# Sixteen matmuls of the identity on TensorE ahead of the first projection

## What is computed

```python
Q = (x @ Wq.T).reshape(b, n, H, R); K = (x @ Wk.T).reshape(b, n, H, R)
V = (x @ Wv.T).reshape(b, n, H, d)
attn = softmax(einsum('bnhr,bmhr->bhnm', Q, K), axis=-1)
x = layernorm(x + einsum('bhnm,bmhd->bnd', attn, V))
h = silu(tlin(x, w1_w, w1_s)) * tlin(x, w2_w, w2_s)
h = gelu(tlin(h, h1_w, h1_s)); h = gelu(tlin(h, h2_w, h2_s))
x = layernorm(x + tlin(h, w3_w, w3_s))
```

## Time and profile before

| | |
|---|---|
| median of three runs | 1031.53 us (1029.31 to 1032.75) |
| the profiled execution | 1031.28 us, its span 1029.4 us |
| TensorE busy | 984.3 us (96%) |
| ScalarE, VectorE, GpSimd busy | 859.1, 827.1, 513.0 us |
| mean granted TensorE clock | 0.980 |

### The profile page before, as it was taken

How to read it: one execution, slowest core, us unless ns; L and a number is a source line. 1 busy time by engine, 2 the same in 40 slices (tenths; PEclk the granted TensorE clock), 3 DMA queues, 4 the chain that set the end, 5 groups by cost and what they waited for, 6 DMA issues and landing times.

```text
span 1029.4 us, 19535 instructions
## 1 busy us (share of the span) xinstructions
PE 984.3 (96%) x6465; PEld 816.5 (79%) x6465; DVE 827.1 (80%) x1827; ACT 859.1 (83%) x1992; POOL 513.0 (50%) x509
## 2 busy tenths in 40 slices
PE   4887999999999999999999999999999999999976
PEld 3676888888888888888888888888888888888844
DVE  4695778887888988788898878889887888878754
ACT  5574998989899898989989898998989899898632
POOL 1591545544455554545555454555545454554623
PEclk9898999999999999999999999999999999999978
DMA  5000000000100000010000001000000100000000
GB/s 184 11 3 21 2 11 12 21 11 2 31 2 22 12 21 11 1 32 2 21 12 21 12 2 32 2 22 11 22 11 2 32 1 12 11 12 11 12 0 21
DMA packets 21749, 17.81 MB, mean 17 GB/s; under 512 B 1040, under 2 KB 17936, under 8 KB 21648
## 3 DMA queue, kind: packets, MB, share of 16 engines
q1 hardware_dynamic: 21648, 16.53, 5.3%
HBM read 12.33 MB, written 4.19 MB: 16 GB/s over the span
## 4 chain that ended last, share of the span: by engine, by line
PE 91%; DVE 4%; ACT 2%; issue 2%; DMA 0%; POOLq 0%; SPq 0%; DVEq 0%; POOL 0%; ACTq 0%
PE bank L852 13%; PE bank L958 13%; PE bank L959 13%; PE bank L846 12%; PE bank L848 11%; PE bank L847 11%; PE bank L891 11%; PE bank L938 3%; PE bank L939 3%; ACT prob L383 1%; DVE pt_lo L196 1%; DMA wk_in<-in_wk_t 0%; DVE neg_max L600 0%; DVE t_lo L196 0%; DVE v_lo L196 0%
## 5 line engine op out<-in xcount | busy, mean ns | idle before, releaser
L248 POOL TENSOR_TENSOR prob<-prob,inv_total 128x512 f32<-128x512 f32 x256 | 267.8, 1057 | 185.0 <-DVE inv_total L606 185.0
L383 ACT ACTIVATE prob<-bank,neg_max 128x256 f32<-128x256 f32 x512 | 237.9, 480 | 4.1 <-DVE neg_max L600 3.4
L196 DVE TENSOR_TENSOR pt_lo<-bank,pt_hi 128x512 fp32r<-128x512 f32 x256 | 175.4, 685 | 46.3 <-ACT pt_hi L199 41.8
L199 ACT ACTIVATE pt_hi<-bank 128x512 fp32r<-128x512 f32 x256 | 154.2, 602 | 66.9 <-PE bank L852 64.5
L600 DVE TENSOR_REDUCE neg_max<-bank 128x2 f32<-128x512 f32 x256 | 171.4, 681 | 24.7 <-PE bank L891 24.7
L852 PE MATMUL bank<-ident,prob 128*128 128x128 f32 x1024 | 157.7, 277 | 7.2 <-issue 4.7
L852 PEld LDWEIGHTS bank<-ident,prob 128*128 128x128 f32 x1024 | 120.9, 141 | 39.9 <-issue 9.6
L846 PE MATMUL bank<-pt_hi,v_hi 128*128 128x256 f32 x512 | 151.9, 297 | 0.0
L848 PE MATMUL bank<-pt_hi,v_lo 128*128 128x256 f32 x512 | 145.3, 284 | 0.0
L847 PE MATMUL bank<-pt_lo,v_hi 128*128 128x256 f32 x512 | 145.3, 284 | 0.0
L196 POOL TENSOR_TENSOR even_lo<-gelus,even_hi 128x512 fp32r<-128x512 f32 x48 | 61.8, 1288 | 103.7 <-DVE even_hi L678 103.7
(11 more groups left out here) (101 smaller groups left out, 2357.2 us busy)
## 6 DMA issues: line engine op xcount, KB each, us to landing
xt_in<-in_x_t SPq DMA_DIRECT2D x16, 256.0 KB, 2.7
res<-in_x SPq DMA_DIRECT2D x16, 256.0 KB, 2.8
out_x<-y SPq DMA_DIRECT2D x16, 256.0 KB, 2.3
h_in<-in_h_t SPq DMA_DIRECT2D x2, 1024.0 KB, 9.2
w_in<-in_w_t SPq DMA_DIRECT2D x3, 256.0 KB, 5.9
wv_in<-in_wv_t SPq DMA_DIRECT2D x1, 512.0 KB, 5.9
wq_in<-in_wq_t SPq DMA_DIRECT2D x1, 256.0 KB, 3.1
wk_in<-in_wk_t SPq DMA_DIRECT2D x1, 256.0 KB, 5.1
```

Source lines behind the costliest of these rows:

```text
L196: return eng.tensor_tensor(dst, src, hi.bitcast(F32), ALU.subtract)
L199: return nc.scalar.activation(dst, src, ACT.Copy)
L248: nc.gpsimd.tensor_tensor(prob[:, s, :, :], prob[:, s, :, :], inv_total[:, u, :].unsqueeze(2).to_broadcast([P, NT, N]), ALU.mult).then_inc ...
L383: last = nc.scalar.activation(prob[:, slot(i, u, RING), nt, :], sc[u % 2][:, nt * N:(nt + 1) * N], ACT.Exp, bias=neg_max[:, u, nt:nt + 1], ...
```

## The change

Ahead of TensorE's wait for the query and key weights, a wait for the identity is put in, and then sixteen matmuls of the identity with itself, all into the first 128 columns of bank 3. Their results are not read; the bank is written anew from its start by the groups that use it later. The operands are plain f32, not fp32r. `WARM` is 16.

```diff
@@ -17,6 +17,7 @@
 HALF = KC // 2
+WARM = 16
@@ -1079,6 +1080,10 @@
                 turn_flag(k)
 
+
+            pe.wait_ge(s_ident, 1)
+            for n in range(WARM):
+                mm(bank[3][:, 0:P], ident[:, :], ident[:, :], start=True, stop=True)
             pe.wait_ge(s_wqk_lo, 2)
             query_or_key(0, 0)
             query_or_key(0, 1)
```

## The result

| | median | runs |
|---|---|---|
| before | 1031.36 us | 1029.31 to 1032.83 (15) |
| changed | 1026.62 us | 1025.15 to 1028.91 (15) |

The ratio is 0.9955, with a 95% interval of 0.9947 to 0.9963: faster by 4.7 us, where 1.75 us were forecast. The profiled execution of the changed kernel took 1027.0 us, its span 1025.2. The page of the profile shows it hardly at all: TensorE's busy time is 2.6 us longer, with 32 more matmuls, and the granted clock has the same look as in the earlier trace rows.

What follows compares the result with a forecast made beforehand. TensorE was taken as the bound from 100 us on, so only the start could gain: 1031.28 less 1.75 us for a fast start, zero for later cold stretches, gives 1029.5 us; range 1026.5 to 1032.6.

Steps and rivals of the forecast that it cites:

- The sixteen are hidden: At the start, the sixteen matmuls run beside the weight transfers from 1.6 to 7.1 us, 0.43 each before the clock rises.
- the upper end: Highest price considered for each new matmul: four turns, 0.85 us at the lower clock, 13.6 us for all sixteen.
- The clock holds until 8.79: Full clock survives the 1.7 us of TensorE idle time left before the first real matmul at 8.79 us.
- The path to `neg_max`: With full clock from 8.79 us, VectorE's `neg_max` starts near 13.1 in place of 14.87, 1.75 us earlier.
- 1.75 us should pass whole into the stretch where TensorE is full: No transfer holds the chain behind `neg_max`, so the start's 1.75 us gain reaches the stretch from 100 us on.
- The later cold stretches: Low clock at 22.9 to 26.3 and 33.1 to 39.9 us: effect taken as zero, ends -4.0 to +1.5.
- The end of -4.0: Most favourable effect allowed on the low-clock stretches at 22.9 and 33.1 us: 4.0 us gained.
- The end of +1.5: Least favourable effect allowed on the low-clock stretches at 22.9 and 33.1 us: 1.5 us lost.
- Rival A: Earlier work also escapes the low clock at 22.9 us or part of that at 33.1; 1027.0 us, chance 0.22.
- Rival B: The sixteen matmuls at the start do not raise the clock, so nothing changes; 1031.4 us, chance 0.13.
- Rival C: The sixteen matmuls are dear and delay the first real matmul; 1031.3 to 1036 us, chance 0.20.
- within 0.3%: Whole kernel: time between 1028.4 and 1034.6 us, counted as no change against before; chance 0.70.

Runs made afterwards that it cites:

- h_warm8: The changed kernel with the branch condition turned round and 8 matmuls ahead in place of 16; ratio 0.9940 to the kernel before.
- e1: The kernel before with sixteen plain f32 matmuls at the end of the branch never taken, so later code lies 64 instructions further; ratio 0.9971, median 1027.8 us.
- e4: The changed kernel with the branch condition turned round, so the executed path stands directly behind the branch; ratios 0.9917 and 0.9914, medians 1023.0 and 1022.2 us.
- f1: The kernel before with only the branch condition turned round, without the sixteen matmuls; ratio 0.9929 to the kernel before.
- e2: The changed kernel with 48 such matmuls in the branch never taken, 256 instructions in all; ratio 0.9978 to the kernel before, median 1028.8 us.
- e3: The changed kernel with sixteen matmuls of one column each in place of 128; ratio 0.9980 to the kernel before, median 1029.2 us.
- f2: The changed kernel with 32 turns of the identity (transposing mode) in place of the sixteen matmuls; ratio 0.9960 to the kernel before.
- f4: The changed kernel with the branch turned round and plain identity matmuls filling TensorE's idle places up to the branch; ratio 0.9870, median 1017.3 us.
- h_warm32: The changed kernel with the branch condition turned round and 32 matmuls ahead in place of 16; ratio 0.9931 to the kernel before.

## Why the prediction was right and wrong

**The sixteen are hidden: right.** They started at 1.51 for 1.6 and ended at 7.3 for 7.1. The price of 0.43 us, chosen between 0.21 and 0.85, was good. The profile has one line for the first part of them and one for the last (duration in ns, lowest, median, highest; from 1.5 to 5 us and from 6 to 7):

```profile
L1086 PE MATMUL bank<-ident x16: 421/421/579, 1.5 to 4.9; 128*128 128x128 f32 x16
```

```profile
L1086 PE MATMUL bank<-ident x11: 275/275/275, 5.8 to 6.9; 128*128 128x128 f32 x11
```

Sixteen of these, eight products, start from 1.5 to 4.9: about 0.45 us for a product. At full clock they start 0.11 us apart, eleven from 5.8 to 6.9 (1.1 us over ten steps), 0.22 for a product. Four turns in place of one, the upper end, was twice too dear. The Trainium skill, "TensorE: Matmul & The Clock Gate", section Terms, gave that price; the trace has two turns in place of one.

**The clock holds until 8.79: right**, over 1.46 us. With the eight of h_warm8 it did not: after 3.13 us without work the clock was still up, and fell 0.7 us later in the midst of work.

**The path to `neg_max`: right**, 13.10 for 13.1, the gain 1.77 us for 1.75. The step from `neg_max` to the second scores (13.10 to 15.89) is 2.79 us, as before (14.87 to 17.66).

**"1.75 us should pass whole into the stretch where TensorE is full": right for the 1.75 as far as the runs can tell, but the step was taken as if nothing else changed.** Against a kernel with the same code position the fast start is worth 1.7 us (change against e1), 1.2 and 1.5 (e4 against f1); each is uncertain by 1.5 to 2 us. The term that failed is missing in the sum: what sixteen matmuls are as *code*. I counted their time and nothing for the 64 instructions that all later code moved by, although the row that would have shown it was in the trace of before, idle time with "issue" as its releaser in the middle of a group of three, at 85.54. It measured 3.1 us between the profiles and 3.0 us by itself in e1 (about 2.4 as the difference of the change's ratio and e2's). 1.37 of it are the stop; the rest is the clock. TensorE's matmuls of 256 columns stand 0.21 us apart at the lower clock and 0.12 at the higher. The lower one lasts until about 91.1 in the kernel before, 5.6 us after TensorE resumed from the second stop, and only until 84.2 in the changed one, 3.8 us after it resumed from the only one. One row of each, in this order:

```profile
90.83 0.55 PE L848 MATMUL bank<-wv_hi,xt_lo 128*128 128x512 f32 x1
```

```profile
84.09 0.33 PE L848 MATMUL bank<-pt_lo,v_hi 128*128 128x256 f32 x1
```

These are the matmuls during which the clock rises. That the stop also kept the clock down is argued from these traces, not shown: wherever the stop is there (before, e2) the distance is 18.5 us or more, wherever it is absent with the branch as it was (after, e1, e3, f2) it is 16.5 to 17.4.

**The later cold stretches: zero was about right for this change** (22.7 to 26.2 and 29.6 to 36.4 us in the changed kernel, as long as before). The end of -4.0 was of the right size for what they cost: filled in f4, they gave 3.8 us up to the flag's turn. The end of +1.5 was not tested. Rival A gave 1027.0, near the time, for another reason than the true one. Rival B falls with the fast start. Rival C's mechanism is shown by h_warm32, but not at sixteen.

Numbers: the forecast of 1029.5 was 2.9 us too high, the range of 1026.5 to 1032.6 holds 1026.6 by a hair, and "within 0.3%" was not what came: 0.45% is clear. That the time lies in the range at all is luck: the range was drawn for the scatter and the cold stretches, and about two thirds of the gain are a term that it didn't know. With the target where it was, the change would be worth what e2 shows, 0.2% (2.3 us).

What stays open: by how much the position of code moves other changes of this kernel, since only two positions were run; and whether the stop by itself keeps the clock down, since no kernel had the one without the other.

## What to carry to other kernels

An edit ahead of a branch has two costs, its time and its length in code; compare kernels with a branch only after the path taken stands directly behind it, or after padding the path not taken. Idle time put down to "issue" inside a group of matmuls that waits for nothing may be a load of code: look for a packet on the instruction queue ahead of the moment at which the engine resumes (2.4 to 2.8 us here). Where TensorE waits on short dependent steps, its idle places also cost time through the low clock that follows them: filled, those of the first cycle and of the tail gave about 5 us each. Matmuls without a reader, put ahead of the wait into a free bank and short enough to end before it, cost nothing that these runs show; 32 in place of sixteen at the start ended too late and cost 1.8 us.

## What the runs showed of the hardware

- A plain f32 matmul of 128x128 by 128 columns is two weight loads and two matmuls, and takes 0.45 us at 1.2 GHz and 0.22 at 2.4.
- A taken branch cost TensorE 3.6 us of load (4.85 of idle time against 1.25). A second stop of 1.37 us (before) and 0.91 us (e2) stood twelve instructions behind the target; moving the code by 64 instructions took it away (e1), by 256 brought it back (e2).
- From a 16 KB packet on the instruction queue to the next matmul it took 2.7 and 2.8 us at the two stops of the kernel before, and 2.4 at the second stop of e2.
- Sixteen products of one column kept TensorE occupied for 7 us and did not raise the clock; 32 turns did.
- The clock can fall while TensorE works, 0.7 us after it resumed from 3.13 us without work (h_warm8).
